# Attention and routed FFN on one core: the products for the maximum go ahead of those for the exponentials in each step

## The reference

```python
def _L0_xattn_ref(q, k, v):
    qh = q.reshape(b * h, d // h, m)
    kh = k.reshape(b * h, d // h, -1)
    vh = v.reshape(b * h, c // h, -1)
    qk = jnp.einsum('bdm,bdn->bmn', qh, kh) * scale
    sm = jax.nn.softmax(qk, axis=-1)
    return jnp.einsum('bmn,bcn->bcm', sm, vh).reshape(b, c, m)
...
x = x + _L0_xattn_ref(_layernorm(x, axis=-1), ctx_2048, ctx_2048)
x = x + _L0_ffn_ref(_layernorm(x, axis=-1), gate, w0, w1, wo)   # 8 experts, the best 2 of each row
```

## Time and profile before

| | |
|---|---|
| median of 3 runs | 527.05 us (524.05 to 527.81) |
| the profiled execution | 521.89 us |
| its span | 520.1 us |
| TensorE busy | 432.0 us (83%) |
| VectorE busy | 278.5 us (54%) |
| ScalarE busy | 231.3 us (44%) |
| GpSimd busy | 210.8 us (41%) |
| mean granted clock | 0.918 |

### The profile page before, as it was taken

One profiled execution on the slowest core, in us unless ns is written; L12 is line 12 of the kernel. 1 busy time (PEld: TensorE's weight loads), 2 busy tenths in 40 slices (PEclk: granted clock), 3 DMA queues, 4 the chain that ended last, 5 costly groups with the idle time before them and its releaser, 6 DMA issues.

```text
span 520.1 us, 10170 instructions
## 1 busy us (share of the span) xinstructions
PE 432.0 (83%) x3182; PEld 229.7 (44%) x3183; DVE 278.5 (54%) x594; ACT 231.3 (44%) x456; POOL 210.8 (41%) x221
## 2 busy tenths in 40 slices
PE   0336999889898899498547999999999999999991
PEld 0301333334343343133323666665665566556650
DVE  7569998896988899336895222222222222222220
ACT  0432798886887889376202222222222222222220
POOL 4452412264435327340722344344434543454422
PEclk9955899997999999869757999999999999999997
DMA  8899559787679737932781123222322232223321
GB/s 265 215 299 256 145 152 221 216 254 218 181 200 259 220 115 261 348 110 86 256 310 31 32 43 56 43 40 41 50 50 40 40 50 51 40 40 46 50 25 20
DMA packets 45208, 69.91 MB, mean 134 GB/s; under 512 B 6887, under 2 KB 34200, under 8 KB 45176
## 3 DMA queue, kind: packets, MB, share of 16 engines
q1 hardware_dynamic: 29698, 41.37, 28.0%
q0 software_dynamic: 11424, 24.39, 20.2%
q10 hardware_dynamic: 4054, 3.72, 2.5%
HBM read 42.57 MB, written 26.58 MB: 133 GB/s over the span
## 4 chain that ended last, share of the span: by engine, by line
PE 61%; DVE 13%; DMA 9%; ACT 5%; SPq 4%; POOL 3%; issue 3%; POOLq 0%; DVEq 0%; ACTq 0%
PE max_ps L1366 26%; PE pv_ps L1264 7%; PE ring_ps L1378 6%; PE pv_ps L1378 6%; DVE mx L871 5%; PE ring_ps L1247 5%; ACT pt L723 5%; DMA Q<-mrow 4%; PE ring_ps L1339 3%; PE max_ps L1159 2%; SPq L369 2%; PE ring_ps L1329 2%; DMA Q<-q_img 1%; PE ring_ps L1230 1%; DMA q_img<-qpart 1%
## 5 line engine op out<-in xcount | busy, mean ns | idle before, releaser
L871 DVE TENSOR_REDUCE mx<-max_ps 128x4 f32<-128x1024 f32 x128 | 149.4, 1216 | 19.9 <-PE max_ps L1159 19.9
L723 ACT ACTIVATE pt<-ring_ps 128x512 f32<-128x512 f32 x256 | 139.1, 598 | 37.5 <-PE ring_ps L1247 34.1
L1366 PE MATMUL max_ps<-w_sb,pt 128*128 x312 | 142.1, 598 | 0.9 <-ACT pt L794 0.9
L665 POOL DMA_INDIRECT out<-rb,sidx x39 | 62.0, 1591 | 120.0 <-DVE gidx L1100 58.9
L1124 DVE TENSOR_TENSOR pt<-pt,max_ps 128x512 f32<-128x512 f32 x39 | 26.8, 688 | 121.8 <-PE max_ps L1366 62.9
L1366 PEld LDWEIGHTS max_ps<-w_sb,pt 128*128 128x128 f32 x312 | 56.9, 192 | 58.3 <-issue 58.2
L1264 PE MATMUL pv_ps<-pt,w_sb 128*27 128x256 f32 (+2 forms) x1024 | 81.5, 403 | 1.2 <-ACT pt L723 0.6
L1159 PE MATMUL max_ps<-K,Q 48*128 48x256 bf16 x512 | 54.4, 295 | 18.9 <-DVE mx L871 10.5
L1247 PE MATMUL ring_ps<-Q,K 50*128 50x256 f16 x512 | 53.0, 287 | 19.2 <-ACT pt L723 10.1
L801 ACT ACTIVATE pt<-ring_ps 128x512 f32<-128x512 f32 x39 | 23.3, 597 | 71.9 <-PE ring_ps L1339 71.9
L657 POOL DMA_INDIRECT pt<-xrow,gidx x39 | 38.7, 992 | 29.1 <-issue 11.0
(11 more groups left out here) (162 smaller groups left out, 392.2 us busy)
## 6 DMA issues: line engine op xcount, KB each, us to landing
w_sb<-in_L_ffn_w_kernel POOLq DMA_DIRECT2D x16, 512.0 KB, 7.8
K<-k_img SPq DMA_DIRECT2D x16, 448.0 KB, 6.3
Q<-q_img SPq DMA_DIRECT2D x16, 448.0 KB, 7.5
q_img<-qpart SPq DMA_DIRECT2D x32, 192.0 KB, 3.8
k_img<-kpart SPq DMA_DIRECT2D x28, 192.0 KB, 3.9
wo_sb<-in_L_ffn_wo_kernel POOLq DMA_DIRECT2D x8, 512.0 KB, 11.3
acc<-pvs SPq DMA_DIRECT2D x7, 512.0 KB, 3.1
q_sb<-in_x SPq DMA_DIRECT2D x16, 128.0 KB, 4.5
```

Of the source, the lines that this page charges most:

```text
L665: g.indirect_dma_start(xacc, bass.IndirectOffsetOnAxis(ap=sidx[sl.par][:, 0:1], axis=0), y_sb[sl.par], None, compute_op=ALU.add).then_inc( ...
L723: a.activation(pt[:, (2 * i + h) % PTN, :, :], bank(key)[:, :, :], ACT.Exp, scale=SCALE).then_inc(ring_read, 1)
L871: v.tensor_reduce(mx[:, t % 2, :, :, p].rearrange("q mt h -> q h mt"), max_ps[n % 2][:, :, :, :], axis=AX.X, op=ALU.max).then_inc(max_read, 1)
L1366: last = nc.tensor.matmul(flat(max_ps[sl.par][:, bank_of]), lhsT=xT[sl.par][:, k * P:(k + 1) * P], rhs=weight(w, e, KC, k), start=(k == 0) ...
```

## The change

In the loop of TensorE, `scores_max(i + LEAD)` stands in front of `scores_exp(i)`, and no longer behind `turn_max`. Nothing is added or taken away, and the other engines' code is the same.

```diff
             for i in range(-LEAD, STEPS):
                 t, p = i // PAIRS, i % PAIRS
+                if i + LEAD < STEPS:
+                    scores_max(i + LEAD)
                 if i >= 0:
                     scores_exp(i)
                 if p == TURN and 0 <= t + 1 < T:
                     turn_max(t + 1)
-                if i + LEAD < STEPS:
-                    scores_max(i + LEAD)
                 if (t, p) in v_at:
                     make_v(v_at[t, p])
```

## The result

The changed kernel takes 529.19 us (median of 20 runs) where the kernel before takes 525.92 us (20 runs on the same chips); the ratio is 1.0121, with a 95% interval of 1.0098 to 1.0145. The ratio leaves out one run far off (868.88 us) and three that were over 1.5% above the fastest. The two medians are only 3.3 us apart, 0.6%, where the ratio stands for 6.3 us; a second set of runs gives a ratio of 1.0102 and medians 5.0 us apart (529.23, 524.28). The direction is clear of the noise, the size is known as 3 to 6 us. The first profile shows 3.5 us of the cost, the second 5.9.

What follows compares the result with a forecast made beforehand. No engine had room in the attention, so the last-ending wait at each place was taken to decide. Terms from start to tile 13 summed to 8.2 us, giving 535.2 us on the median of 527.05; range 524 to 541.

Steps and rivals of the forecast that it cites:

- The start: Step 0: first exponential product stands behind a maximum product held by VectorE; 1.1 us lost, bounds 0.6 and 1.4.
- `pv` loses its cover: Pairs 4, 6 and 0: `pv` waits 0.13 us for ScalarE, formerly covered by the maximum product; 0.4 us an ordinary tile.
- What pair 2 gives back: Pairs 2 and 3: maximum product runs inside waits for ScalarE; the end of the tile gains nothing.
- VectorE's wait holds the exponentials: Pair 2, odd tiles: next exponential product 1.82 us behind late maximum product, 0.93 later; 0.5 to 0.8 us a tile.
- Steps with inserted work: Behind `make_v` and `logits`: maximum product ahead of a late exponential product; 0.14 us for each such place.
- Where transfers decide: Pair 0 of tiles 4, 10, 14: stalls hide earlier losses; tile 10 adds 0.6 us, tile 14 nothing.
- The clock: Rival: new idle pieces halve TensorE's clock in the body for another 14 us; +12 to +18 us; chance 0.11.
- hidden: Rival: VectorE's earlier feeding and transfers absorb the waits, leaving the start and few places; +0 to +4 us; chance 0.27.
- Faster: Rival: VectorE sets the pace of tile pairs, earlier maximum products shorten seven by 0.6 us; -3 us; chance 0.12.

Runs made afterwards that it cites:

- late `pv`: Each `pv` product one pair later, ten buffers of exponentials for eight; ratio to the kernel before 0.9984 in the old order, 1.0147 in the new.
- the weights behind the norm: First sixteen expert-weight loads moved behind the norm of tiles 10 and 11; ratio to the kernel before 1.0099 in the old order, 1.0161 in the new.
- mixed order: Changed kernel with old order at pair 2, or pairs 2 and 3, of odd tiles from 5: ratios 1.0006, 1.0004; with start and `pv` also undone: 1.0047.
- lead of 17: The kernel before with a lead of 17 pairs for 16 and no other change of order; ratio to the kernel before 1.0157.

## Why the prediction was right, and which terms were not

The forecast was 1.6% slower (8.2 us). Measured is 1.2% (6.3 us) by the ratio, 0.6% (3.3 us) by the medians. The direction held, and the main waits are there as described; their sum was too large, and the total came near in part by luck. Step by step:

- *The start*, 1.1 us: measured 1.0 us at pair 3 of tile 0 (54.48 for 53.47), 0.9 us at pair 3 of tile 1. Over all profiles step 0 starts at 48.4 to 48.8 us in the old order and at 49.6 to 50.4 in the new.
- *`pv` loses its cover*, 0.13 us at pairs 4, 6 and 0, 0.4 us a tile: `pv` waits 0.13 us at pair 4, the steps of pairs 4, 6 and 0 are 0.09, 0.11 and 0.13 us longer, a tile 0.33 us, and the runs with late `pv` show that this wait is the whole of it. In time they show nothing, since the transfer for tile 14 took back what the tiles gave. The reason given for leaving out pair 2 was wrong: its `pv` reads results as old as at the other even pairs. It loses nothing because `pv` stands behind the turn and, now, behind the copy of `pv_ps`: it starts 1.07 us behind the exponential product in both orders (62.56, 63.63 and 63.42, 64.49).
- *What pair 2 gives back*, nothing: held. From pair 2 to pair 3 it is 1.96 us in both orders.
- *VectorE's wait holds the exponentials*, M + 1.82 instead of M + 0.89: measured 1.84. The way of a tile, which includes `pv`'s waits, is 0.9 us longer in tiles 5 and 9 by the second profile (forecast 0.8 each), 0.6 in tile 13 (0.5), 0.3 instead of 0.7 in tile 11. The first two profiles give no comparison for tile 7, with half clock in the old one; 12.25 us in the changed kernel against 12.33 in the old order with the weights behind the norm speaks against 0.8 there. Tile 13 is the cleanest: in all profiles without late `pv` or a mixed order VectorE lets go 0.27 us earlier, and the exponential product of pair 3 comes 0.86 us later behind it. In time the steps at pairs 2 and 3 of odd tiles are the dearest part: without them the kernel can't be told from the one before.
- *Steps with inserted work*, 0.14 us for each: this term was wrong. The tile with values lost 0.29 us, the ordinary one 0.33: the step of `make_v` is 0.07 us longer, and the wait of 0.11 us at pair 6 is gone. Only with late `pv` does it cost its 0.13 us. The same holds behind the logits: tiles 8 and 12 lost 0.17 and 0.22 us (second profile), not 0.53.
- *Where transfers decide*, tile 14 at nothing: this was the term most off. The stall gave back 3.0 and 3.5 us in the two profiles. Tile 10, at 0.6 us more, came out 0.3 us shorter in the first profile, with 1 us of half clock in it.
- *The clock* had been a rival with 0.11, on top of the sum. It came as a part: the changed kernel had 0.96 and 0.94 in the body where it was 0.98. Tile 7 of before, which holds nearly all of a half clock of 6.8 us, takes 14.56 us; without one, in the old order with the weights behind the norm, it takes 12.33, so such a stretch costs 2.2 us, and 2.7 by the 0.39 above. That is 2 to 3 us between the first two profiles. Five profiles of the new order have 10.2 to 20.5 us of half clock in eleven tiles, three of the old 3.4 to 10.2. That the waits for VectorE cause it is argued only: it fell less in the kernel without them (6.8 us), but the new order with late `pv` has these waits and 3.4 us, and the lead of 17 has no new order and 17.1. The traces show a link, though: TensorE is idle for over 1 us at a time 27 times between 58 and 206 us of the fourteen profiles, 26 of them ahead of a maximum product that waits for VectorE, and 14 times the clock falls shortly after (idle from 107.0 for 2.09 us and the fall at 110.2 in the first profile of the changed kernel). It falls 32 times in all, so in more than half of the cases no such piece comes before it, and what makes it fall there stays open.

So the waits cost some 3.3 us of the 6.7 at pair 3 of tile 13 (1.0 at the start, 0.3 in tile 2, 2 in the body), where the sum had 8.2; the clock took most of the rest, and the transfer gave 3 back. That the total lies near the forecast is in part luck: terms that were too large stood in for a clock that the sum didn't have. By size the waits are what *hidden* gave (0 to 4 us, with the start and a few places left), though at the steps themselves the waits are the forecast's. *Faster* fails on the tiles: of those where both first profiles are at full clock (2, 3, 4, 9, 12 and 13) only tile 4 gets shorter, and it had waited for a transfer. No kernel here is clearly faster than the one before: those that equal the kernel before do so by undoing the change in odd tiles, or never had it.

## What to carry to other kernels

When two independent pieces of work stand in one engine's queue, the one between a producer and the consumer of its results is cover; before moving it, look up in a stretch without it how long the consumer then waits. A piece that may wait for a slow engine must not stand ahead of the one that feeds the busy engine, however useful its head start is elsewhere: undoing the change at ten of 128 steps was enough to bring the time back. And compare two kernels at the same clock, since a difference of 2 us in waits came with 2 to 3 us of clock. Last, before a stall is bought off, ask what its traffic will meet next; here the same 6 MB of weights met the maxima of tile 14, those of tile 15, or the denominators, and the time never fell.

## What the runs showed of the hardware that was not expected

An 8 KB transfer took from 9.0 to 18.5 us beside the weights in ten profiles, and 3.7 us when the weights were held back. It was longest where the first weights had been issued only 5.7 us ahead of it, but at almost the same distance (8.4 to 8.6 us ahead) it took 9.5 and 15.0 us (the changed kernel, and the same with late `pv`), and the cause of the spread stays open.

The granted clock fell to half for 3.4 to 10 us at a time in the body of every one of these kernels, where TensorE is busy for about 90% of the time (117.9 of 130.3 us in the kernel before), and with no idle piece there longer than 2.6 us.

Two profiles of one kernel agree to 0.01 us in tiles 2, 3, 12 and 13, and are 2.3 us apart at pair 3 of tile 13. For a change of a few tenths of a microsecond in a tile, the tiles at full clock are the measurement, and the total is not; where VectorE is the late one, even such a tile varies by 1 us.
